# A graph-transformer layer on one core: row maxima two steps behind their queries, both query tiles in one VectorE reduction over two PSUM banks, eight probability buffers

## The reference, cut to what matters

```python
xn = layernorm(x)                                   # 1250 nodes, 512 features
x = x + graph_conv(xn, src, dst) + linear_attention(xn)
z = layernorm(x)
e_s, e_t = argmax(router(mean(z)))                  # one of 4 spatial, one of 4 temporal experts
spatial = mha(ln_s(z), expert=e_s) @ W_so + b_so    # 8 heads of 64, full softmax over 1250 keys
xt = ln_t(z)
temporal = xt + causal_mha(xt, expert=e_t) @ W_tp + b_tp
fused = mha(q=spatial, kv=temporal)                 # 8 heads, full softmax
z2 = z + fused @ W_co + b_co
return x + z2 + gelu(ln_m(z2) @ W1.T + b1) @ W2.T + b2
```

## Time and profile before

| | before |
|---|---|
| median of 3 runs | 1874.95 us (1872.63 to 1875.15) |
| the profiled execution | 1872.27 us |
| span of its trace, first to last instruction | 1870.2 us |
| mean granted TensorE clock in it | 0.966 of full speed |
| TensorE busy | 1660.2 us, 89% |
| VectorE busy | 1299.5 us, 69% |
| ScalarE busy | 711.6 us, 38% |
| GpSimd busy | 679.1 us, 36% |

### The profile page before, as it was taken

One profiled execution on the slowest core, in us unless ns is written; L12 is line 12 of the kernel. 1 busy time (PEld: TensorE's weight loads), 2 busy tenths in 40 slices (PEclk: granted clock), 3 DMA queues, 4 the chain that ended last, 5 costly groups with the idle time before them and its releaser, 6 DMA issues. The chain is left out here.

```text
span 1870.2 us, 32821 instructions
## 1 busy us (share of the span) xinstructions
PE 1660.2 (89%) x10735; PEld 1382.3 (74%) x10735; DVE 1299.5 (69%) x2681; ACT 711.6 (38%) x1346; POOL 679.1 (36%) x815
## 2 busy tenths in 40 slices
PE   2899988876899999998998988899999996899998
PEld 1788657755777777777877777778877875697896
DVE  7778768885768667875665766777878798673332
ACT  1223211024755445555555542355645453120110
POOL 3213001102546344352433236133343367373440
PEclk9999999987999999999999999999999998899999
DMA  3101000011031000030000000000000002121111
GB/s 114 35 7 46 12 6 25 16 56 40 13 128 46 23 18 7 7 123 12 13 12 13 7 1 18 23 12 13 7 12 7 7 1 84 39 67 40 45 34 55
DMA packets 24795, 58.11 MB, mean 31 GB/s; under 512 B 2538, under 2 KB 4806, under 8 KB 24014
## 3 DMA queue, kind: packets, MB, share of 16 engines
q1 hardware_dynamic: 24650, 56.18, 9.3%
HBM read 44.87 MB, written 11.30 MB: 30 GB/s over the span
## 5 line engine op out<-in xcount | busy, mean ns | idle before, releaser
L1794 DVE TENSOR_REDUCE max_part<-ps 125x2 f32<-125x500 f32 x520 | 327.7, 672 | 113.9 <-PE ps L2330 99.2
L1373 ACT ACTIVATE p_raw<-ps 125x500 f32<-125x500 f32 x520 | 296.8, 586 | 281.4 <-PE ps L2373 273.9
L1081 POOL TENSOR_TENSOR p_sum<-p_sum,p_raw 125x250 f32<-125x250 f32 x200 | 150.4, 752 | 341.2 <-ACT p_raw L1373 339.2
L2388 PE MATMUL ps<-p_raw,v_rows 125*64 125x250 f32 x2080 | 247.6, 379 | 0.0
L2388 PEld LDWEIGHTS ps<-p_raw,v_rows 125*64 125x64 f32 x2080 | 142.9, 137 | 72.3 <-issue 3.5
L2330 PE MATMUL ps<-k_both_a,q_both_a 128*125 128x250 f32 x520 | 144.7, 295 | 37.6 <-issue 22.7
L1634 DVE TENSOR_SCALAR onehot<-iota_h,win_key,key_t 125x320 f16 x453 | 174.8, 386 | 0.5 <-issue 0.4
L2272 PE MATMUL ps<-xa_hi,w_hi 128*128 128x418 f32 (+1 forms) x448 | 152.3, 340 | 24.5 <-POOL w_lo L947 9.0
L2369 PE MATMUL ps<-q_both_a,k_both_a 128*125 128x250 f32 x520 | 154.0, 316 | 15.6 <-issue 12.1
L1633 DVE TENSOR_SCALAR onehot<-iota_h,low_t 125x125 f16 x453 | 130.9, 289 | 47.3 <-issue 27.8
L2369 PEld LDWEIGHTS ps<-q_both_a,k_both_a 128*125 128x125 f32 x520 | 98.1, 189 | 71.4 <-issue 60.5
(11 more groups left out here) (396 smaller groups left out, 3856.4 us busy)
## 6 DMA issues: line engine op xcount, KB each, us to landing
w_raw<-in_w_mlp SPq DMA_DIRECT2D x32, 256.0 KB, 2.6
w_raw<-in_w_gps SPq DMA_DIRECT2D x16, 256.0 KB, 2.6
w_raw<-in_w_tp SPq DMA_DIRECT2D x16, 256.0 KB, 2.6
w_raw<-in_w_sp SPq DMA_DIRECT2D x12, 256.0 KB, 2.7
w_raw<-in_w_cr SPq DMA_DIRECT2D x12, 256.0 KB, 2.7
d_xt<-xb_hi SPq DMA_DIRECT2D x1, 2508.0 KB, 9.4
d_xt<-xb_lo SPq DMA_DIRECT2D x1, 2508.0 KB, 15.0
xa_hi<-d_xt SPq DMA_DIRECT2D x1, 2508.0 KB, 9.7
```

Of the source, the lines that this page charges most:

```text
L1081: pool.tensor_tensor(total, total, halves[0], ALU.add).then_inc(s_add_a, 1)
L1373: act.activation(p_raw[:, g % PR, :], ps[0:TOK, g % 2, 0:4 * TOK], ACT.Exp, scale=SCALE).then_inc(s_exp, 1)
L1794: dve.tensor_reduce(part[:, y, :, j], ps[0:TOK, bank, 0:4 * TOK].rearrange("p (h k) -> p h k", h=2), AX.X, ALU.max)\
L2388: ins = pe.matmul(ps[r, bank, 0:2 * TOK], v_rows[:, n % 2, kt, h, :], p_raw[:, (g - 1 + h) % PR, cols], start=(b == 0 and x == 0), stop=last)
```

## The change

**Maxima in pairs.** An M task is now `("M", n, i, j)`: for one key block TensorE computes both query tiles into two neighbouring banks (4 and 5, or 6 and 7; four matmuls), and VectorE reduces both banks in one instruction, 125 x 1000 to 125 x 4. There are 260 of them. `bank_plan` takes the pair whose later use lies longer ago and that holds no K, Q or F of the same step. At most one M stands in a step (`COST` 0.48 instead of 0.24).

**Later behind their queries.** An M may stand no earlier than two steps behind its Q (one in unit 2 of causal passes), instead of one; three behind the last K instead of two; R one step further behind the last M. The due steps of Q and M lie earlier.

**VectorE's order in a step.** The second head's additions come first, then the low parts of K and Q of the step before.

**Buffers.** `p_raw` has eight buffers instead of six. To make room, the plane `o_plane` is split into `o_hi` and `o_lo`, which lie on memory that is free at that time.

```diff
-PR = 6
+PR = 8
 def maxima(n, i):
-    return [("M", n, i, y, j) for y in range(2) for j in range(blocks_in(n, i))]
+    return [("M", n, i, j) for j in range(blocks_in(n, i))]
...
-COST = {"K": 2.3, "V": 2.3, "Q": 1.4, "M": 0.24, "R": 0.2, "T": 0.7, "F": 3.0}
+COST = {"K": 2.3, "V": 2.3, "Q": 1.4, "M": 0.48, "R": 0.2, "T": 0.7, "F": 3.0}
...
-                due[task] = gf - 7 - 2 * (len(tasks) - 1 - x) // 3
-            due["Q", n, i] = gf - 10 - 2 * len(tasks) // 3
+                due[task] = gf - 8 - 4 * (len(tasks) - 1 - x) // 3
+            due["Q", n, i] = gf - 13 - 4 * len(tasks) // 3
...
+def query_lag(n, i):
+    return 1 if CAUSAL[n // 4] and i == 2 else 2
...
-        free = LAST[(x - 3) // 5, (x - 3) % 5] - 1 if x >= 3 else 0
+        free = LAST[(x - 3) // 5, (x - 3) % 5] - LEAD if x >= 3 else 0
...
     if kind == "M":
-        return max(later(("Q", n, rest[0]), 1), later(("K", n, 2), 2))
+        return max(later(("Q", n, rest[0]), query_lag(n, rest[0])), later(("K", n, 2), 3))
     if kind == "R":
-        return later(maxima(n, rest[0])[-1], 2)
+        return later(maxima(n, rest[0])[-1], 1 + query_lag(n, rest[0]))
...
+        elif kind == "M":
+            free = [x for x in range(SIDE_BANKS_AT, 8, 2) if not any(held.get(x + y, "-")[0] in "KQF" and at[held[x + y]] >= slot for y in range(2))]
+            x = min(free, key=lambda x: max(order.get(x, -1), order.get(x + 1, -1)))
+            use = [x, x + 1]
+            order[x] = order[x + 1] = len(banks)
...
# VectorE
-                dve.tensor_reduce(part[:, y, :, j], ps[0:TOK, bank, 0:4 * TOK].rearrange("p (h k) -> p h k", h=2), AX.X, ALU.max)\
+                dve.tensor_reduce(part[:, :, :, j], ps[0:TOK, bank:bank + 2, 0:4 * TOK].rearrange("p y (h k) -> p y h k", h=2), AX.X, ALU.max)\
...
                 for g in range(first, end):
+                    if STEP[g][3] == 1:
+                        add_second_head(g)
                     if g > first:
                         for task in SIDE[g - 1]:
                             last_out(task)
-                    if STEP[g][3] == 1:
-                        add_second_head(g)
```

More of the change, by code:

```diff
@@ L284, in plan_steps @@
                     continue
-                if task[0] in LINEAR and g < linear_at + 2 or used.count(task[0]) >= (2 if task[0] == "M" else 1):
+                if task[0] in LINEAR and g < linear_at + 2 or task[0] in used:
                     continue
@@ L562, in build @@
         q_row = [sb(f"q_row_{x}", [128, QR, 2 * TOK], F32R) for x in "ab"]
+        v_rows_at = place["end"]
         v_rows = sb("v_rows", [TOK, 2, NT, 2, 64], F32)
@@ L1884, in _ @@
                 query_lo(n, 0)
[L1885 removed]
+                for task in largest[:3]:
                     maximum(*task[1:])
                 query_lo(n, 1)
[L1888 removed]
+                for task in largest[3:]:
                     maximum(*task[1:])
                 for g in range(first, end):
+                    if STEP[g][3] == 1:
+                        add_second_head(g)
                     if g > first:
```

42 lines of the change are left out of this document (22 added, 20 removed).

## The result

The changed kernel takes 1883.0 us, the median of six runs (1879.6 to 1886.7), beside 1873.6 us for six runs of the kernel before: ratio 1.0051, 95% interval 1.0037 to 1.0065. It is slower by some 9.5 us. The forecast was 1868, faster; 1883 lies inside the range that was given, on the side of rival A.

The account below looks back on a forecast made before the run. TensorE was taken as the bound, 1044.9 of 1152 us busy in the attentions, leaving about 107 us of standstill to win or lose. Terms summed to -7 us, 1868 for the median; range 1848 to 1892.

Parts of the forecast that it names:

- rival A: Pairs' banks become the wait through VectorE's queue ahead of reductions, at 54 places; 1890 us with 0.5 us queue; chance 0.32.
- Maxima two steps behind: First maxima no longer wait for their query's low parts on TensorE: gain 14 us, bounds 10 and 18.
- R one step earlier: Three waits of scores for row maxima behind K tasks end: gain 7 us, bounds 4 and 8; R's own waits, gain 2.
- One reduction over two banks: Joint reduction takes 1194 ns, saving 17 us of VectorE's time, off the path; the stage gains 1 us.
- VectorE's order: Additions ahead of low parts fill VectorE's waits instead of following them: gain 1 us, bounds 0 and 10.
- Banks in pairs: Pairs come free later: linear tasks +13 us, maxima -2, value turns +3, a query's bank +1; bounds +5 and +42.
- maxima that take a bank from other maxima -2: Waits among maxima: 13 at 0.75 us each, 10 us, and 35 at 5 together, against 17.2 paid before: -2.
- a query's bank that the next M wants, +1: Maxima waiting for a bank a query still holds: cost 1 us, within the bounds for banks in pairs.
- Scores with nothing between: Scores following scores rise from 27 to 39 places, each waiting for its exponential; twelve at 0.2 us: +3.
- rival C: Gain comes back as scores waiting for exponentials, 8 us, shown by a rise over 10 us; 1876 us; chance 0.18.
- Eight buffers: Exponentials wait next to nothing for a probability buffer, so two more buffers gain and lose nothing.
- B: VectorE's queue clears, so most of 24 us of waits for reductions go; 1852 us; chance 0.14.

Follow-up runs that it names:

- experiment 3: VectorE's order undone: changed kernel with low parts first 1899.4 us; kernel before with additions first 1870.3; changed order of tasks, single banks, low parts first 1856.7.
- experiment 2: Kernel before with the pairs alone (one step behind the query, due steps and VectorE's order as before, six buffers): 1948.4 us, ratio 1.0402.
- experiment 4: Changed kernel, three variants: freely chosen single banks with own reductions 1847.0 us; neighbouring banks, split reduction 1853.5; pairs kept, banks chosen by expected free time 1894.8.
- experiment 6: Changed kernel with six probability buffers instead of eight: 1881.1 us, ratio 1.0036 to the kernel before.

## Why the prediction failed, point by point

The runs give a chain from the kernel before to the changed one. The first step is several edits together, each later one a single edit; a difference of two such ratios is uncertain by some 4 us:

| step | ratio to before | us |
|---|---|---|
| later maxima, in the changed kernel's order of tasks, single banks, eight buffers, low parts first | 0.991 | -16.9 |
| additions first | 0.9863 | -8.8 |
| neighbouring banks | 0.9891 | +5.2 |
| one reduction for both | 1.0051 | +30.0 |

In another order the steps would share the sum otherwise: the additions are worth 16 us with pairs (experiment 3), and the pairs cost 75 us one step behind the query (experiment 2).

**Maxima two steps behind** (-14). Right: the first maxima were late by 13.6 us less. Maxima without a releaser came to 8.5 us in the profile, where some 12 were expected.

**R one step earlier** (-7). Right where it looked: the three waits of 2.3 us are gone, and the scores of the causal passes are late by 8.7 us less. What it did not look at is the next task but one: in passes 4 to 7 maxima right behind are now late by 2.0 to 2.3 us, 8.3 together, for the bank of the Q task that stands in front of them.

**One reduction over two banks** (1194 ns, VectorE's share 1 us). Right: 1197 ns, and the reductions cost VectorE 309.8 us where they cost 327.7, 17.9 less against 17. Whether the stage gained the 1 us by it cannot be told from these runs. The prediction set against this the Trainium skill's page "VectorE: DVE Perf Modes", section "The DRAIN you can't avoid", which says that the next operation does not start until the pipe has emptied. The same paragraph adds that an operation which is not held starts earlier, and the four reductions in 2.43 us and the 17.9 us agree with that; so the 39 us that the prediction read out of the page need not be its price for this case.

**VectorE's order** (-1, bounds 0 and 10). The mechanism was named, the size was wrong: 16 us with pairs, outside the bounds, and 9 with single banks, at their end. I counted the additions that fill a wait and not the reductions queued behind additions and low parts alike.

**Banks in pairs** (+14, with the reduction's own -1 in it). This is the step that failed, though not at the linear tasks, where it put most of its price. That part was right in count and price: 35 places were forecast to be 0.57 us short. In the order of the changed kernel 30 of them have one step's scores and one M in between; these 30 are late by 0.58 us on average, and all 35 by 19 us together, against 20. At the third place of the section on the change it reads like the sum:

```profile
1451.91 0.27 PE L2345 MATMUL ps<-k_both_b,q_both_b 128*125 128x250 f32 x1
...
1452.22 1.20 DVE L1807 TENSOR_REDUCE max_part<-ps 125x4 f32<-125x1000 f32 x1 [0.82 <-PE ps L2345]
...
1453.48 0.46 PE L2285 MATMUL ps<-xa_hi,w_hi 128*128 128x418 f32 x1 [0.38 <-DVE max_part L1807]
```

The reduction starts 0.31 us behind the last matmul's start, as it does with an empty queue in the earlier trace rows, and the K task is 0.53 us late. For maxima that take a bank from other maxima -2 was right too (-1.8).

What was too small is the term "a query's bank that the next M wants, +1". By the count maxima that take a bank from a K, Q or V task became late by 10.7 us more, and those that take one from an R task, which the sum put at nothing, by 4.0. A task in one bank closes both banks of a pair, but that is the smaller part of it: with single banks in the same order the two are late by some 10.4 and 7.2 us, and with the later maxima alone by 8.7 and 8.3, where the changed kernel has 14.3 and 7.6 and the kernel before 3.6 and 3.6. So most of it belongs to the later maxima, and came without any pair.

What the pairs themselves cost shows only against single banks in the same order: 35 us, 30 of them for the one instruction, where the sum had 14. The linear tasks, where more than half of the 30 stand (experiment 4), cost what was forecast for them; the rest is more than the sum had. The sum subtracted the waits that the kernel before paid, 6.8 and 17.2 us. But the second of these falls by itself with the later maxima and single banks: maxima that take a bank from other maxima are late by 15 us there instead of 26, and by 24 with the pairs. So the -1.8 is a win of the later maxima that the pairs mostly took back, and the later maxima and VectorE's order together won 26 us in the chain, where the sum had 21 (the +3 of the scores counted in). From the first matmul of an M to the end of its reduction, each bank of a pair is held 2.47 us, and 2.02 with two reductions; that gap is what one instruction for both adds, at four banks that all side tasks share.

**Scores with nothing between** (+3). The mechanism was right and the size a third of what it was: late scores in the full passes rose by 9.1 us. I counted 12 more places at 0.2, but 27 and 39 are the places where three scores stand in a row. Directly behind a score stand 41 more in these passes, and some 22 more of them are late by over 0.15 us. Waits of the scores for exponentials, which rival C had asked for, rose by more than 10 us:

```profile
PEld ps L2384 <- ACT p_raw L1386: 37.4, 68, 3.0
```

With single banks in the same order they are 36.7 and the kernel is 26 us faster than before. So C is there, by its own test, and does not decide.

**Eight buffers** (0). Right.

**The rivals.** A named what costs: one instruction holds both banks, and its split is worth 30 us. But A had the loss in the queue ahead of the reductions at 54 places, and by its own test it fails: linear tasks' weight loads wait 19.9 us for reductions, the "some 20" of the forecast and not over 30. At the places that A names the sum was about right (19 us at the linear tasks against 20, 15 at the 13 maxima with one pair left against 10). The loss against the forecast stood elsewhere: at maxima that want a bank of a query or an R task, which the profile shows as waits for a query's low part, and at scores. So it is in part luck that the time came out on A's side. The Trainium skill's page "PSUM — Partial Sum Buffer" (section "PSUM bank collisions raise a hardware error") asks to guard PSUM by bank and quadrant, or more simply by bank, and not by address. In all kernels here a side task holds whole banks, so no run shows what another guard would do. B fell, since waits for reductions rose.

At products and denominators (0) the count has +4.7. About half of it stands at the one place, described below, where the clock fell; the rest is open.

## What to carry to other kernels

Merging two instructions on an engine that does not set the time saved nothing here, and it cost where it made TensorE wait for both results: price a merged read by how long it holds its buffers, from the first write to the last read, and count every kind of task that takes one of them, not only the kind that was merged. Where a change has several parts, price each against the kernel that has the others already: a wait that one part is credited with may be gone through another, and a merge can cost back what another part had won. Price the short places one by one; neither an empty queue nor an average tells them. From the last matmul's start to the reduction's start it is 0.31 us with an empty queue, 1.48 on average in the kernel before and 0.85 in the changed one, while the linear tasks that the forecast counted were late as if the queue were 0.1 us longer than empty. A win of two microseconds at one task is only one if no later task waits as long for what was moved in front of it.

## What the runs showed of the hardware

**The clock can fall inside matmuls that are busy all the time.** The last fold task of pass 1 is 32 matmuls of two columns. In the profiled execution of the changed kernel the granted clock fell to the lower level, 1.2 GHz, 1.1 us after its first matmul, and stayed there through the denominators and products behind. Up to then the matmuls start 0.11 us apart, and 0.21 from there on. The windows after (PE, PEld, DVE, ACT, POOL busy, then the granted clock):

```profile
676.00:679.60 3.60, 2.99 (x28) 2.79 (x26) 2.94 (x4) 2.15 (x5) 1.99 (x3) 1.00 0.02 5
679.60:689.90 10.30, 10.30 (x50) 8.11 (x50) 3.59 (x7) 0.21 (x1) 0.00 (x0) 0.50 0.00 0
```

The kernel before, the same 32 matmuls and then the 4 us behind them:

```profile
674.00:678.00 4.00, 4.00 (x36) 3.84 (x36) 2.48 (x5) 0.51 (x1) 0.99 (x2) 1.00 0.00 0
678.00:682.00 4.00, 4.00 (x25) 2.58 (x24) 1.55 (x5) 1.06 (x2) 0.63 (x1) 0.62 0.01 2
```

There they ran at the full clock, 2.4 GHz, and it fell only behind them. Half of 10.3 us is 5.2, and 0.38 of 4 us is 1.5, so by this estimate it costs some 3.6 us more here; over the stage both kernels have the same mean, 0.98. It is not the order of tasks that does this. With six buffers (experiment 6) the order is the same and TensorE waits the same 0.6 us in front, but there the 32 matmuls ran at the full clock almost to their end, and the 3.7 us behind them look like those of the kernel before:

```profile
676.60:680.30 3.70, 3.70 (x36) 3.69 (x35) 1.59 (x3) 0.00 (x0) 0.00 (x0) 0.97 0.02 4
680.30:684.00 3.70, 3.70 (x21) 2.08 (x20) 2.50 (x5) 0.00 (x0) 0.00 (x0) 0.57 0.00 0
```

So the same order of tasks lost the clock here for longer in one execution and for shorter in the other, and what decides it stays open. The 3.6 us may be a part of the 4.9 by which the profiled execution lies above the median; that is not shown.

**An addition on VectorE waits for GpSimd.** In the changed kernel an addition of two tiles in SBUF (line 1834) takes 0.42 us in the median and 1.39 at most. At the first place of the section on the change, where a unit's first maxima still wait 2.11 us, VectorE and GpSimd were doing this:

```profile
804.98 1.45 POOL L960 TENSOR_TENSOR w_lo<-w_raw,w_hi 128x512 fp32r<-128x512 f32 x1
805.34 1.37 DVE L1834 TENSOR_TENSOR p_sum<-p_sum,p_raw 125x250 f32<-125x250 f32 x1
...
806.74 0.47 DVE L1789 SCALAR_TENSOR_TENSOR q_both_a<-ps,sp_vecs,q_both_a 64x250 fp32r<-64x250 f32 x1
...
807.81 0.35 PE L2345 MATMUL ps<-k_both_a,q_both_a 128*125 128x250 f32 x1 [2.11 <-issue]
```

The addition ends 0.28 us behind the GpSimd operation that runs beside it, and the low part of the query, which ScalarE has evicted by 805.54, starts 1.2 us after that, behind the addition. It is no single case: 17 additions of lines 1832 and 1834 in this trace take over 1 us, and every one ends 0.27 or 0.28 us behind a GpSimd operation that was running when it started. The Trainium skill, page "SBUF — State Buffer", section "Terms", says that the two engines share a pair of ports that one instruction holds to its end; this place agrees.
